# Second, third and last stage in one block, with tile 0's products of the third stage ahead of the second stage's last convolutions

## The reference

```python
x = x + L0_ffn(L0_cond(x))  # cond: a 64x64 mixture kernel of each batch; ffn: top-1 of 8 low-rank experts
x = x + L1_ffn(L1_cond(x))  # cond: grouped convolution, 9 taps, + context; ffn: int8 product 1024x1024 of quantised rows
x = x + L2_ffn(L2_cond(x))  # cond: as L1's; ffn: below
x = x + L3_ffn(L3_cond(x))  # cond: as L0's; ffn: below

# L2_ffn(x)
base_out = x @ base_w.T + base_b                 # 1024 x 1024
res_hidden = x @ A.T                             # 64 numbers a row
probs = softmax(x @ router_w.T)                  # 16 experts, the two largest kept, weights normalised
delta = einsum(combine, res_hidden, B)           # combine: weight of each expert for each row
return base_out + 0.5 * delta

# L3_ffn(x)
routing = top_k(x @ gate_w, 2)                   # of 8
shared = relu(x @ up_w) ** 2 @ down_w            # 1024 -> 2048 -> 1024
routed = (x @ fc1 @ expert_w) * sum(routing) @ fc2
return layernorm(shared + routed) * gamma + beta
```

## Time and profile before

| | us |
|---|---|
| three runs | 1875.67, 1877.85, 1879.64 |
| the profiled execution, own time | 1875.55 |
| its span | 1873.8 |
| TensorE busy | 1718.3 (92% of the span) |
| VectorE, ScalarE, POOL busy | 796.2, 476.8, 388.1 |

### The profile page before, as it was taken

How to read it: one execution, slowest core, us unless ns; L and a number is a source line. 1 busy time by engine, 2 the same in 40 slices (tenths; PEclk the granted TensorE clock), 3 DMA queues, 4 the chain that set the end, 5 groups by cost and what they waited for, 6 DMA issues and landing times. The chain is left out here.

```text
span 1873.8 us, 22327 instructions
## 1 busy us (share of the span) xinstructions
PE 1718.3 (92%) x8396; PEld 1412.2 (75%) x8396; DVE 796.2 (42%) x1453; ACT 476.8 (25%) x710; POOL 388.1 (21%) x218
## 2 busy tenths in 40 slices
PE   7899748998599999999769999999999999999995
PEld 3578637878478888888648888888777888888874
DVE  4256589984443334332213333333344333333324
ACT  2344314423211111111023223222144222232123
POOL 1000011233123434333311111111144111111115
PEclk9999969999699999999979999999999999999998
DMA  8376314556513332333642111111194111111104
GB/s 306 100 190 191 124 47 146 163 197 210 203 52 112 105 116 83 102 116 105 201 138 68 45 45 45 56 56 45 48 300 141 51 45 45 45 45 45 68 34 157
DMA packets 126804, 205.81 MB, mean 110 GB/s; under 512 B 14436, under 2 KB 82092, under 8 KB 126124
## 3 DMA queue, kind: packets, MB, share of 16 engines
q1 hardware_dynamic: 109716, 158.41, 26.5%
q0 software_dynamic: 13568, 35.65, 6.0%
q10 hardware_dynamic: 3456, 10.88, 1.7%
HBM read 143.01 MB, written 61.89 MB: 109 GB/s over the span
## 5 line engine op out<-in xcount | busy, mean ns | idle before, releaser
L1278 PE MATMUL pd<-down_hi,hid_hi 128*128 128x512 f32 x640 | 249.2, 389 | 2.9 <-issue 2.9
L1278 PE MATMUL pu<-l_base_hi,up_hi 128*128 128x512 f32 x640 | 249.3, 390 | 0.0
L1278 PE MATMUL pu<-l_base_lo,up_hi 128*128 128x512 f32 x640 | 249.1, 389 | 0.0
L1278 PE MATMUL pd<-down_lo,hid_hi 128*128 128x512 f32 x640 | 249.1, 389 | 0.0
L1278 PE MATMUL pd<-down_hi,hid_lo 128*128 128x512 f32 x640 | 249.1, 389 | 0.0
L1278 PE MATMUL pu<-l_base_hi,up_lo 128*128 128x512 f32 x640 | 249.1, 389 | 0.0
L1402 POOL TENSOR_TENSOR down_lo<-raw,down_hi 128x1024 fp32r<-128x1024 f32 x40 | 99.6, 2490 | 692.3 <-ACT down_hi L1416 692.3
L1551 DVE TENSOR_TENSOR hid_lo<-hidden,hid_hi 128x512 fp32r<-128x512 f32 x64 | 44.3, 692 | 381.2 <-ACT hid_hi L1466 381.2
L1497 DVE TENSOR_TENSOR acc<-pd,acc 128x512 f32<-128x512 f32 x224 | 143.5, 685 | 54.8 <-PE pd L1278 51.5
L1460 ACT ACTIVATE hidden<-pu 128x512 f32<-128x512 f32 x64 | 38.3, 598 | 462.7 <-PE pu L1278 462.7
L1278 PEld LDWEIGHTS pd<-down_hi,hid_hi 128*128 128x128 f32 x640 | 120.1, 188 | 28.5 <-issue 3.7
(11 more groups left out here) (244 smaller groups left out, 2890.1 us busy)
## 6 DMA issues: line engine op xcount, KB each, us to landing
X<-scratch_x SPq DMA_DIRECT2D x256, 64.0 KB, 2.6
l_x<-scratch_x SPq DMA_DIRECT2D x32, 512.0 KB, 5.7
raw<-in_up SPq DMA_DIRECT2D x32, 512.0 KB, 3.6
raw<-in_down SPq DMA_DIRECT2D x32, 512.0 KB, 3.7
x_in<-in_x SPq DMA_DIRECT2D x16, 512.0 KB, 4.1
scratch_x<-x_in SPq DMA_DIRECT2D x16, 512.0 KB, 3.6
scratch_x<-l_x SPq DMA_DIRECT2D x16, 512.0 KB, 4.8
scratch_y2T<-y2T SPq DMA_DIRECT2D x16, 512.0 KB, 3.0
```

Source lines behind the costliest of these rows:

```text
L1278: mm = pe.matmul(out, lhs[a], rhs[b], start=first and n == 0, stop=last and n == len(pairs) - 1)
```

## The change

The second, third and last stage become one block. Each of the phase functions now gives back one function for each engine, and `build` calls the three in turn in each engine's stream. No barrier and no clearing of semaphores is left between them; where one stage must not overwrite what another still reads, there is now a wait on one semaphore of the other (`prior[...]`, `first[...]`). The buffers of all stages are laid out anew by hand (`persistent_buffers`, `l0_buffers`, `l1_buffers`, `l2_buffers`, `l3_buffers`), so that tile 0's inputs of the third stage and the first weights of the last one have a place beside those still in use.

In the parts:

- Second stage: `LATE` is 8. ScalarE loads the router weights at its start, loads tile 0's y2 at s = 13 and rounds it at s = 14, POOL makes its low part at s = 15. The convolutions of tiles 14 and 15 leave the stage's loop; TensorE, VectorE, ScalarE and SyncE do their parts of it inside s = 0 and 1 of the third stage. SyncE stores x2 of tile 15, then loads B, then the windows of tile 15.
- Third stage, opening: TensorE does router product, turning, first half of base for tile 0, router product of tile 1, second half of base, then the convolution of tile 14, the turning of cr, and after the product with B the convolution of tile 15. ScalarE rounds all eight slices of B in one go behind the exp of s = 0; VectorE subtracts all eight at the start of s = 1, and adds tile 14's context behind them. The bodies of s = 1 end, on VectorE and ScalarE, with a wait until all of y2T is stored.
- Third stage, loop: POOL makes the low part of y3 ahead of x3b, and SyncE stores in that order too.
- Third stage, end: SyncE loads the first two up slices in s = 16, ScalarE and VectorE split the first of them in s = 17; POOL loads the first column group of y as before, the second one only when tile 14's y3 is stored.
- Last stage, opening: the order is gate product of group 0, up 0, up 2 (both read group 0), gate product of group 1, up 1, turning of the gate, up 3.
- Layer norm: VectorE computes (acc - mean) * gamma into scratch while ScalarE squares into PSUM (banks `pu`), and then scratch * rstd + x3b in one instruction. ScalarE loads x3b, POOL only stores. VectorE finishes the tile before the last one ahead of the last add.

```diff
-    LATE = 9
+    LATE = 8
...
+            if s == NT - 3:
+                act.wait_ge(turned, len(GROUPED))
+                act.wait_ge(y2_stored[0], 16)
+                ahead["y2_load"](act)
+            if s == NT - 2:
+                act.wait_ge(peaked, 3 * len(GROUPED))
+                ahead["y2_high"](act)
...
+        x2_out(NT - 1)
+        sp.wait_ge(f_mm, 2 * NT)
+        for h in range(2):
+            sp.dma_start(K["B_raw"][:, 4 * h:4 * h + 4, :], A["l2_B"][:, 4 * h:4 * h + 4, :]).then_inc(K["low_loaded"], 16)
+        windows_in(NT - 1)
+        store_y2(sp, NT - 4)
+        store_y2(sp, NT - 3)
...
+            if isinstance(s, int) and s == 1:
+                prior["shift_tile"](act, NT - 1)
+                act.wait_ge(prior["conv_done"], 2 * NT)
+                act.wait_ge(prior["y2_made"], 2 * NT)
+                for slot in prior["y2_stored"]:
+                    act.wait_ge(slot, 16 * NT // 2)
...
+            if isinstance(s, int) and s == 1:
+                low_rest(0, KC)
+                prior["conv_out"](dve, NT - 2)
...
+            if has[1]:
+                base_half(1, s).then_inc(base_mm, 1)
+                if not later(s, 2):
+                    prior["conv"](pe, NT - 2)
+                    pe.wait_ge(prior["scaled"], NT)
+                    turn_cr(s)
...
+            if isinstance(s, int) and s == 1:
+                prior["conv"](pe, NT - 1)
+                pe.wait_ge(prior["y2_made"], 2 * NT)
...
             if isinstance(s, int) and s == NT:
                 pool.wait_ge(base_mm, NT)
                 pool.wait_ge(y3_stored, 32 * (NT // 2 + 1))
-                    for n in range(2):
-                        for part in range(2):
-                            pool.dma_start(base[part][...], SC["y3s"][part][...])
+                first["y"](pool, 0)
+            if has[2]:
+                pool.wait_ge(y3_hi, s - 1)
+                pool.tensor_tensor(y3s[1][:], y3[:], y3s[0][:].bitcast(F32), ALU.subtract).then_inc(y3_lo, 1)
+            if isinstance(s, int) and s == NT:
+                pool.wait_ge(y3_stored, 32 * NT)
+                first["y"](pool, 1)
...
+            if isinstance(g, int) and g == 0:
+                gate_block(0)
+                upward(g, 0, half)
+                upward(g, 2, half)
+                gate_block(1)
+                upward(g, 1, half)
+                turn_gate()
+                upward(g, 3, half)
...
+        def centre(T):
+            dve.scalar_tensor_tensor(out=scratch[:], in0=acc[:, T % HT, :], scalar=nmean[:, T:T + 1], in1=gamma[:],
+                                     op0=ALU.add, op1=ALU.mult).then_inc(weighed, 1)
+        def finish(T):
+            dve.reciprocal(inv[:, T:T + 1], root[:, T:T + 1]).then_inc(inverted, 1)
+            dve.scalar_tensor_tensor(out=acc[:, T % HT, :], in0=scratch[:], scalar=inv[:, T:T + 1], in1=x3b[:, T % 2, :],
+                                     op0=ALU.mult, op1=ALU.add).then_inc(out_made, 1)
```

More of the change, by code:

```diff
@@ L33 @@
 KR = BATCH + NK
+SMALL = D + NT * EG + 7 * NT
 def stepped(eng, body, depth):
@@ new lines, in l3_buffers @@
+def l3_buffers(nc, s_):
+    names = {}
+    names["dn"] = [[s_.split(f"down{v}{i}", [P, D]) for i in range(2)] for v in range(2)]
+    names["hid"] = [s_.split(f"hid{v}", [P, 2, NT // 2 * P]) for v in range(2)]
+    up0, raw0 = s_.split("up0", [P, D]), s_.sb("raw0", [P, D])
+    names["scratch"] = s_.sb("scratch", [P, D])
+    names["logits"], names["top"] = s_.sb("gate_logits", [P, NT // 2 * EG]), s_.sb("gate_top", [P, NT // 2, EG])
+    names["gate_sum"], names["sums"] = s_.sb("gate_sum", [P, NT]), s_.sb("row_sums", [P, NT, 2])
+    names["rows"] = [s_.sb(n, [P, NT]) for n in ("neg_mean", "sum_sq", "root", "rstd")]
+    up1, raw1 = s_.split("up1", [P, D]), s_.sb("raw1", [P, D])
+    names["up"], names["raw"] = [up0, up1], [raw0, raw1]
+    names["acc"] = s_.sb("acc", [P, NT // 2, D])
+    names["x3b"] = s_.sb("l3_x3b", [P, 2, D])
+    names["act_f"], names["gamma"] = s_.sb("hidden", [P, 2, HALF]), s_.sb("gamma", [P, D])
+    names["pu"] = s_.ctx.enter_context(nc.psum_tensor("pu", [P, 4 * HALF], F32))
+    names["pd"] = [s_.banks(f"pd{v}_", 2) for v in range(2)]
+    return names
@@ new lines, in body @@
+            if isinstance(s, int) and s == NT:
+                pool.wait_ge(y3_stored, 32 * NT)
+                first["y"](pool, 1)
+            if has[1]:
+                pool.wait_ge(x3_made, 2 * s)
+                pool.wait_ge(x3b_stored, 16 * s)
+                if not later(s, 2):
+                    pool.wait_ge(beta_loaded, 16)
+                    pool.wait_ge(prior["conv_done"], 2 * NT)
+                pool.tensor_tensor(x3b[:], x3[:, 1 - u, :], beta[:], ALU.add).then_inc(x3b_made, 1)
@@ L1643, in build @@
+                        upward(g, q, half)
+                    if back:
+                        downward(g, u, 2 * q)
+                        downward(g, u, 2 * q + 1)
+        steps(body)(pe)
+    return dict(sync=sync, gpsimd=gpsimd, scalar=scalar, vector=vector, tensor=tensor, prime=prime,
+                first=dict(raw=first_raw, y=first_y, up_hi=first_up_hi, up_lo=first_up_lo))
 def build(nc, A, out):
```

1906 lines of the change are left out of this document (985 added, 921 removed).

## The result

The changed kernel takes 1855.66 us (median of 4 runs, 1852.6 to 1859.6), the kernel before 1878.74 beside it. The ratio is 0.9884, interval 0.9868 to 0.9900: faster by 1.2%, some 23 us. The forecast was 1833 with a range up to 1851. The direction was right, and half of the gain is missing. The profiled execution took 1855.62, its span is 1853.8: 20.0 us less than before, where 45.0 were forecast.

The account below looks back on a forecast made before the run. TensorE, busy 1718.3 of 1873.8 us, was taken as the bound. −24.1 (first seam) + 1 − 14.8 (second seam) + 0.7 − 7.8 = −45.0 from 1875.55 gave 1830.5, with 2.3 for other runs 1833; range 1817 to 1851.

Parts of the forecast that it names:

- the pair of terms for the two long stretches: Third stage's loop stays at 26.4 us a tile; last stage after its opening gains only 0.7 us at the half's end.
- a sign of being wrong: Third stage's loop: the prediction said it would be wrong if the tiles were longer than 26.4 us.
- The held ScalarE: Loop's first tile: ScalarE, held until tile 15's y2 is stored, asks for tile 2's y2 at 510.3; 0.5 us lost.
- The first seam: Between second and third stage: tile 0's products ahead of tiles 14 and 15's convolutions; net −24 us, bounds 12 to 39.
- the tail: After the last matmul: the final store is issued at 1859.1 instead of 1866.88; −7.8 us (−5 to −8.6).
- the stretch up to the first seam: Up to tile 13's convolution: base weights split one tile earlier, one more POOL subtraction; +1 us (−1 to +3).
- the collision with POOL: First seam: one POOL addition (x2 of tile 0) slows VectorE's subtractions of B by 2.1 us.
- Second seam: Into the last stage: y loaded in halves, opening reordered, pauses of 3.9 and 5.1 us; −14.8 us, bounds 3 to 26.
- The rival of the transfers that don't collide: Both seams: y's second half comes by 947.9 and B's split is done sooner; 1820 us, 18 in 100.
- Half's end: Last stage, middle: TensorE's wait for the last add grows from 1.59 to 2.3 us; +0.7 (0 to +3).
- The new waits last longer: Both seams: B lands 8 us later and y's second half behind everything; 1853 us, 16 in 100.
- POOL's new order: Third stage's loop: y3's low part ahead of x3b delays VectorE's next x3; 67 us lost, 1900 us, 3 in 100.

Follow-up runs that it names:

- e9: The changed kernel with 480 unused bytes behind eps and 64 among the small buffers, so operand distances are 0 modulo 512: 1835.45 us, ratio 0.9769.
- e2: The kernel before with 32 unused bytes behind the base weights, nothing else: 1898.91 us, ratio 1.0125.
- e8: The changed kernel, padded (96 bytes behind eps, 64 among small buffers), with ScalarE at tile 1's end waiting only for tile 14's y2 store: 1849.21 us.
- e12: e9 with the base weights loaded one tile earlier still (LATE 7 instead of 8): 1828.82 us.
- e15: The kernel before with 512 unused bytes behind the base weights: 1878.75 us, ratio 0.9988.

## Why the prediction was right or wrong

**The step that failed** is the pair of terms for the two long stretches: the loop kept at 26.4 us a tile and the last stage at its old length plus 0.7. The prediction asked only what could shorten them ("Nothing that other engines do faster can shorten these 1263 us") and not what could lengthen them. It counted the new memory map, which the change names, at nothing. It was not nothing: the loop went up by 10.2 and the last stage by 16.4. Of these 26.6, about 20 are longer steps (0.32 us in each of 14 tiles of the loop, and nearly all of the 16.4). With the distances put back (e9) the program takes 1835.45, 20.2 less, a tile of the loop is back at 26.39, and from the first downward product to the last matmul it is 860.4 us, where the kernel before has 860.1 and the changed one 876.2. e2 shows the cause the other way round. So some 20 us of the missing 23 are this one term, and it was mis-sized at 0. Longer tiles in the loop are a sign of being wrong that the prediction itself named, and it came.

**The held ScalarE** is the second mis-sized term. It was seen and put at 0.5, since the load of tile 2's y2 was to arrive at 513.5, when TensorE would want it at 512.6 to 513. It is 3.48 us of wait and, from 514 to 522, a granted clock of 0.79: the first tile of the loop takes 5.8 us more than before, and e8 takes 5.3 of them back. The load was asked for at 510.10 as forecast, but landed 7.2 us later, not 3.2: tile 2's x, bias and mixture were asked for beside it, at 510.15 to 512.04. In e8, asked for at 500.79 without them, it took 3.2. The price was that of a load by itself.

**What came cheaper** hides part of this. The first seam gave 1.5 more than forecast and the tail 0.9 more, and the stretch up to the first seam lost 1.5 more. That e9 comes within 3 us of 1833 is therefore in part luck: it still has the slow first tile of the loop (31.98).

**First seam.** Forecast from tile 13's convolution to the loop: 49.2, measured 47.7. The total is near by errors that offset. B's loads were taken to start at 458.3 and started at 461.63, and took 14.9 us instead of 13.2, so that its first slice was rounded at 477.6 instead of 472.6. Against that, VectorE's eight subtractions took 9.2 us instead of 11.9, the collision with POOL did not come, nor did the 2.2 us of waiting for tile 1's y2. The prediction saw SyncE's queue reordered, took "less queued on SyncE" for part of 1 us at best, and did not follow the last base slice through that queue. e12 shows 3 to 7 us hanging on it.

**Second seam**: 14.3 gained (59.35 - 45.03) for 14.8. The pause of 3.74 was forecast as 3.9. The second one is 2.83 for 5.1, and not because the load came early: counted from the end of tile 15's work, it landed 0.7 us later than forecast. TensorE came later. From the gate product's start to the second pause it took 19.4 us instead of the 16.3 forecast, at a granted clock of 0.50 from 917 to 921 and 0.73 from 921 to 926. The prediction charged the lower clock behind the second pause only. The rival of the transfers that don't collide did not come. The Trainium skill's "DMA: Bandwidth & Descriptors" (Queues, rings and completion order) says that a DMA engine takes its queues in turns; by the prediction's estimate from it, with turns of equal bytes, tile 14's store would have been done in 8.4 us. Its two parts were issued at 904.84 and 905.47 and landed 12.1 and 13.9 us later, near the 12.2 of the earlier trace rows. The row was the better guide here.

**Half's end and tail.** The wait is 1.92 for 2.3. From the last matmul's end to the last store it takes 5.5 us for 6.1; the tail gave 8.4 us to that store, and 8.7 to the span's end, where 7.8 were forecast.

**Rivals.** "The new waits last longer" would have given 1853, near the measured 1856, and for the wrong reason: apart from the wait for tile 2's y2, the waits were within what was forecast. A time that fits a rival is no proof of it. The loop was indeed longer, but POOL's new order is not it: a tile takes 26.71 us, not the 31.2 of that rival, and in e9, with the new order, 26.39.

## What to carry to other kernels

When a change moves buffers, compare TensorE's busy time at the same number of instructions before anything else; if it rises at full clock, look at the step from matmul to matmul by operand. Keep the two operands of a hot product a multiple of 256 bytes apart within the partition, and put small buffers behind the large ones, or pad their total to a multiple of 256, so that they don't shift one operand against the other. The distances measured are 0, 32, 64, 128, 192 and 224. And where a step is moved in a program, walk every queue it leaves or enters: here the last weight slice, priced by the engines that split it, also cost by its place in SyncE's queue.

## What the runs showed of the hardware that was not expected

- A matmul of 128x512 in a dense stream steps by 0.2268 us or by 0.2333, by the distance in bytes between its stationary and its moving operand: 0.2266 to 0.2268 for the upward product at 0 modulo 256, 0.2327 to 0.2333 for upward and base products at 32, 64, 128 or 224. That is 16 cycles of 2.4 GHz on 544. What in the chip makes it is not shown. The Trainium skill's "TensorE: Matmul & The Clock Gate" (Back-to-back issue gap) gives 518 cycles for 512 columns with a lone gap; no stream here is under 544.
- 32 unused bytes cost the kernel before 20 us of 1879 (e2), and 512 cost nothing (e15).
- crT x B loses less: 0.0022 us a step from the eleventh step of a group on (0.2289 against 0.2267), at a distance of 192.
- At a distance of 0 too, the first ten steps of a group can be longer: 0.2303 for hid x down behind slow upward products in the changed kernel, 0.2267 from the eleventh on.
